# Rows and weights of a graph network turned by VectorE instead of TensorE

## The reference, cut to what matters

```python
# layers 0 and 3 (layer 1 alike, with x @ Wq + bq, no Wo and a mask)
q = x @ Wq.T; k = x @ Wk.T; v = x @ Wv.T + bv
p = softmax(q @ k.T * scale + bias)            # per head
x = layernorm(x + (p @ v) @ Wo.T + bo)
# layer 2, twice
attn = masked_normalised(softmax(h @ h.T / sqrt(D)) * adj)
ctx = (attn * upper) @ (h @ Wl.T) + diag(attn) * (h @ Ws.T) + (attn * lower) @ (h @ Wr.T)
h = relu(layernorm(ctx) * gain + shift)
```

## Time and profile before

| | before |
|---|---|
| median of 3 runs | 2714.04 us (2711.18 to 2718.5) |
| the profiled execution | 2714.95 us, span 2712.9 us |
| PE busy | 2558.7 us, 94% |
| DVE busy | 2079.0 us, 77% |
| ACT busy | 1498.6 us, 55% |
| POOL busy | 1804.6 us, 67% |
| rows turned on PE (L381, L1055), busy | 79.4 + 10.0 + 58.9 us |
| granted TensorE clock, mean | 0.978 |

### The profile page before, as it was taken

One profiled execution on the slowest core, in us unless ns is written; L12 is line 12 of the kernel. 1 busy time (PEld: TensorE's weight loads), 2 busy tenths in 40 slices (PEclk: granted clock), 3 DMA queues, 4 the chain that ended last, 5 costly groups with the idle time before them and its releaser, 6 DMA issues. The chain is left out here.

```text
span 2712.9 us, 65508 instructions
## 1 busy us (share of the span) xinstructions
PE 2558.7 (94%) x22558; PEld 2193.4 (81%) x22558; DVE 2079.0 (77%) x3594; ACT 1498.6 (55%) x3060; POOL 1804.6 (67%) x2045
## 2 busy tenths in 40 slices
PE   7999999996999999969999989999996999999997
PEld 6888888885878888768888878888885888888886
DVE  4788888884888888856666657888886588888887
ACT  4555555553666666535555545666664555555553
POOL 2767777772666666656666647888884567767776
PEclk9999999998999999979999999999998999999998
DMA  3222212213222222132122213232222122212211
GB/s 111 72 70 71 64 60 71 71 47 96 66 78 76 79 74 92 55 111 72 55 75 62 67 60 127 83 93 90 85 86 77 50 72 71 62 62 71 69 58 51
DMA packets 179475, 200.90 MB, mean 74 GB/s; under 512 B 56608, under 2 KB 179360, under 8 KB 179360
## 3 DMA queue, kind: packets, MB, share of 16 engines
q1 hardware_dynamic: 179360, 199.38, 23.6%
HBM read 136.42 MB, written 62.91 MB: 73 GB/s over the span
## 5 line engine op out<-in xcount | busy, mean ns | idle before, releaser
L1095 PE MATMUL l_ps_h<-l_w,l_hT 128*128 128x384 f32 x3456 | 660.3, 342 | 16.5 <-DVE l_hs L1299 14.8
L1095 PEld LDWEIGHTS l_ps_h<-l_w,l_hT 128*128 128x128 f32 x3456 | 592.8, 188 | 63.0 <-issue 33.1
L416 PE MATMUL l_ps_p<-l_xT,l_w 128*128 128x512 f32 x2304 | 604.7, 407 | 6.0 <-DVE l_xT L653 4.5
L343 POOL TENSOR_TENSOR l_pr<-l_sc,l_st 128x768 f32<-128x768 f32 x192 | 283.4, 1476 | 374.7 <-DVE l_st L691 364.3
L416 PEld LDWEIGHTS l_ps_p<-l_xT,l_w 128*128 128x128 f32 x2304 | 418.1, 190 | 95.3 <-ACT l_xT L545 5.3
L313 POOL TENSOR_TENSOR v<-v,l_bvs 128x768 f32<-128x768 f32 x192 | 375.9, 1958 | 0.0
L1182 ACT ACTIVATE l_hlr<-l_ps_h 64x384 f32<-64x384 f32 x512 | 248.7, 486 | 196.8 <-PE l_ps_h L1095 188.8
L698 DVE TENSOR_REDUCE l_st<-l_pr 128x12 f32<-128x768 f32 x192 | 182.8, 952 | 179.0 <-ACT l_pr L609 176.2
L410 PE MATMUL l_ps_p<-l_w,l_xT 128*128 128x384 f32 x1584 | 314.9, 344 | 1.8 <-ACT l_k L566 1.8
L576 ACT ACTIVATE v<-l_ps_p 64x192 f32<-64x192 f32 x704 | 228.9, 325 | 149.7 <-PE l_ps_p L410 142.6
L1003 POOL TENSOR_TENSOR l_hlr<-l_hlr,l_sides 128x768 f32<-128x768 f32 x128 | 243.9, 1905 | 85.0 <-ACT l_hlr L1182 85.0
(11 more groups left out here) (130 smaller groups left out, 4424.7 us busy)
## 6 DMA issues: line engine op xcount, KB each, us to landing
rows<-l_yo SPq DMA_DIRECT2D x256, 192.0 KB, 1.9
l_xa<-rows SPq DMA_DIRECT2D x64, 768.0 KB, 5.0
l_xr<-rows SPq DMA_DIRECT2D x192, 192.0 KB, 2.4
l_xa<-in_x SPq DMA_DIRECT2D x16, 768.0 KB, 4.9
l_xr<-in_x SPq DMA_DIRECT2D x64, 192.0 KB, 2.4
out<-l_yo SPq DMA_DIRECT2D x64, 192.0 KB, 1.9
l_edge<-in_adj SPq DMA_DIRECT2D x80, 128.0 KB, 2.3
raw<-in_L_gnn_Wq SPq DMA_DIRECT2D x3, 576.0 KB, 5.9
```

The costliest lines, as they stand in the source:

```text
L343: nc.gpsimd.tensor_tensor(pr[b][:, :, :], sc[b][:, :, :], st[b][:, 0, :].unsqueeze(2).to_broadcast([P, HEADS, NODES]), ALU.subtract).then_ ...
L416: last = nc.tensor.matmul(bank[:, :], W[m][:, l, t, o * P:(o + 1) * P], rows[:, r, t, :], start=c + t == 0, stop=c == 2 and t == KT - 1)
L1095: last = nc.tensor.matmul(ps_h[m][:, :D], hT[gpar][:, l, t, s * P:(s + 1) * P], W[m][:, r, t, :], start=c + t == 0, stop=c == 2 and t == K ...
```

## The change

The turning moves from TensorE to VectorE. VectorE turns blocks of 32x32, each within its own 32 partitions, so the transfer has to put the right block on the right partitions: partition 32a+c of `xa` takes, for k = 0 to 15, the quarter a of row 32k+c (96 numbers, 384 bytes). One VectorE instruction (`nc.vector.transpose`) on columns 32t to 32t+31 of all 16 k then gives tile t. Features are permuted by this; rows of the weights are permuted alike, which leaves products as they are.

- A group's load is four transfers of 192 KB (2048 runs of 384 bytes) instead of one of 768 KB (512 runs of 1536 bytes). There are two buffers `xa`; SP issues a load up to four (attention) or three (DiGCN) groups ahead, and no longer waits for TensorE.
- Attention: VectorE turns two tiles at the end of s = 0 and one at the end of s = 1 into an SBUF tile `xF`. ScalarE makes the high part from `xF` in s = 1 and s = 2. The low part is now made from two SBUF operands, at the end of s = 2 (two tiles) and s = 3 (one); in l1 by GpSimd, else by VectorE.
- DiGCN: VectorE writes `hF` itself (tile 2 in s = 0 for the next group, tiles 0 and 1 in s = 2 and 3 for the one after). ScalarE's plain copy is gone, and its high part reads `hF`.
- In DiGCN the end of attention step 2 (`attn`, `wide`) moves on VectorE from the end of s = 2 to s = 3, behind L1299.
- Weights: raw matrices come in four transfers each, for the turned ones in runs of 384 bytes, and are turned by VectorE into PSUM. Only Wo is still turned on TensorE, after the first ten projections. At a stage's start the projections wait per matrix.

Diff, cut to its core. Transfers and weights:

```diff
+def spread(src):
+    return src.rearrange("(i k c) (a f) -> i a c k f", k=4 * UNITS, c=32, a=4)
+def blocks(raw):
+    return raw[:, :, :].rearrange("p t n -> p (t n)").rearrange("p (k f) -> p k f", f=D // 4)
...
+                    part = mat.rearrange("(k c) (a f) -> a c k f", c=32, a=4)[a]
+                    sp.dma_start(blocks(self.raw[m])[q, :, :], part).then_inc(self.s_raw[m], 16)
```

In attention (tiles, tables, functions, then VectorE's unit and GpSimd's in l1):

```diff
-        xa = a.sb("xa", [P, UNITS, D])
+        xa = [a.sb(f"xa{b}", [P, 4 * UNITS, D // 4]) for b in range(2)]
+        xF = a.sb("xF", [P, KT, ROWS])
+        AHEAD = (("q", 0), ("q", 1), ("q", 2), ("k", 0), ("k", 1), ("k", 2), ("v", 0), ("v", 1), ("v", 2), ("v", 3))
+        BETWEEN = (((), (0,), (1,)), ((), (2,), (3,)), ((4,), (5,), (6,)), ((7,), (8,), (9,)))
+            def rows_in(g, gpar):
+                if counted(g - 1):
+                    sp.wait_ge(dve_turn, KT * (g - 1))
+                for j in range(4):
+                    sp.dma_start(xa[gpar][32 * j:32 * j + 32, :, :], src_x[g, j]).then_inc(s_xa[gpar], 16)
-            def rows_T(g, t, bank):
-                for u in range(UNITS):
-                    last = nc.tensor.transpose(bank[:, u * P:(u + 1) * P], xa[:, u, t * P:(t + 1) * P], ident[:, :])
-                last.then_inc(pe_x, 1)
+            def rows_turned(g, gpar, t):
+                dve.wait_ge(s_xa[gpar], 64 * (gpair(g, gpar) + 1))
+                if counted(KT * (g - 1) + t + 1):
+                    dve.wait_ge(act_x, KT * (g - 1) + t + 1)
+                    dve.wait_ge(low_x, KT * (g - 1) + t + 1)
+                nc.vector.transpose(xF[:, t, :], xa[gpar][:, :, 32 * t:32 * t + 32]).then_inc(dve_turn, 1)
+            def rows_low(g, gpar, t):
+                dve.wait_ge(act_x, KT * g + t + 1)
+                nc.vector.tensor_tensor(xT[gpar][:, 1, t, :], xF[:, t, :], xT[gpar][:, 0, t, :].bitcast(F32),
+                                        ALU.subtract).then_inc(low_x, 1)
...
                     softmax_sum(n, s)
-                    fill(i, par, s)
+                    for t in ((0, 1), (2,), (), ())[s]:
+                        rows_turned(i + 2, par, t)
+                    for t in ((), (), (0, 1), (2,))[s]:
+                        rows_low(i + 2, par, t)
...
+                        for t in ((), (), (0, 1), (2,))[s]:
+                            rows_low(i + 2, par, t)
```

In DiGCN, in turn on TensorE, ScalarE and VectorE (its start, then its unit):

```diff
-                pe.wait_ge(act_f, KT * (g + 1))
+                pe.wait_ge(dve_turn, KT * (g + 1))
...
-                    nc.scalar.activation(hF[gpar][:, t, :], bank[:, :], ACT.Copy).then_inc(act_f, 1)
-                    nc.scalar.activation(hT[gpar][:, 0, t, :], bank[:, :], ACT.Copy).then_inc(act_x, 1)
+                nc.scalar.activation(hT[gpar][:, 0, t, :], hF[gpar][:, t, :], ACT.Copy).then_inc(act_x, 1)
...
+            weights(LEFT)
+            for t in range(KT):
+                rows_turned(0, 0, t)
+            weights(RIGHT)
+            attention(0, 0, 0)
+            weights(SELF)
...
                     itself(n - 1, 1 - b)
+                    if s == 0:
+                        rows_turned(i + 1, 1 - par, 2)
+                    if s >= 2:
+                        rows_turned(i + 2, par, s - 2)
                     if s == 3:
                         attention(i + 1, 1 - par, 3)
+                        attention(i + 1, 1 - par, 4)
```

More of the change, by code:

```diff
@@ L87, in _ @@
             def _(sp):
-                self.load(sp, first_mats)
+                self.load(sp, first_mats, first_turned)
             @block.gpsimd
@@ L108, in _, with load @@
                     nc.vector.memset(self.v2[b][:, :, :, :], 0.0).then_inc(c_zero, 1)
-    def load(self, sp, mats, free=None):
+    def load(self, sp, mats, turned, free=None):
         for m, mat in enumerate(mats):
@@ L114, in load @@
                 free(m)
-            sp.dma_start(self.raw[m][:, :, :], mat.rearrange("(t p) n -> p t n", p=P)).then_inc(self.s_raw[m], 16)
-            self.loads[m] += 1
+            if m == 3:
+                sp.dma_start(self.raw[m][:, :, :], mat.rearrange("(t p) n -> p t n", p=P)).then_inc(self.s_raw[m], 16)
+                self.loads[m] += 16
+                continue
+            for a in range(4):
+                q = slice(32 * a, 32 * a + 32)
+                if turned:
+                    part = mat.rearrange("(k c) (a f) -> a c k f", c=32, a=4)[a]
+                    sp.dma_start(blocks(self.raw[m])[q, :, :], part).then_inc(self.s_raw[m], 16)
+                else:
+                    part = mat.rearrange("(a t r) n -> a r t n", a=4, r=32)[a]
+                    sp.dma_start(self.raw[m][q, :, :], part).then_inc(self.s_raw[m], 16)
+                self.loads[m] += 16
 class Pass:
@@ L644, in _, with weight_turned @@
             nc.vector.memset(bvs[:, :, :], 0.0).then_inc(c_zero, 1)
-            for step in range(steps):
+            def weight_turned(step):
+                m, t = divmod(step, KT)
+                if not transposed:
+                    return
+                dve.wait_ge(s_raw[m], loaded[m])
+                if step >= 4:
+                    dve.wait_ge(dve_w, step - 3)
+                nc.vector.transpose(w_bank(step)[:, :D], blocks(raw[m])[:, :, 32 * t:32 * t + 32]).then_inc(dve_wt, 1)
@@ L888, in _, with rows_in @@
         def _(sp):
-            sp.dma_start(xa[:, :, :], src_g[0]).then_inc(s_xa, 16)
+            def rows_in(g, gpar):
+                if not inside(g, groups):
+                    return
+                if counted(g - 1):
+                    sp.wait_ge(dve_turn, KT * (g - 1))
+                for j in range(4):
+                    sp.dma_start(xa[gpar][32 * j:32 * j + 32, :, :], src_x[g, j]).then_inc(s_xa[gpar], 16)
+            rows_in(0, 0)
+            rows_in(1, 1)
             sp.dma_start(edge[0][:, :, :], adj_g[0]).then_inc(s_edge[0], 16)
@@ L927, in group @@
                     store(n - 4, s)
-            over_groups(sp, groups, group)
+            over_groups(sp, groups, group, 2)
             if ends:
@@ L1208, in normed @@
                                          scale=ln[b][:, 20:21]).then_inc(act_y, 1)
-            rows_T(0, 0)
+            for step in range(KT):
+                weight_high(step)
+            for t in range(KT):
+                rows_high(0, 0, t)
+            for step in range(KT, 2 * KT):
+                weight_high(step)
             attention(0, 0, 1)
+            for step in range(2 * KT, steps):
+                weight_high(step)
             def group(i, pair, par):
```

366 lines of the change are left out of this document (196 added, 170 removed).

## The result

The changed kernel takes 2730.84 us (median of 5 runs, 2729.26 to 2732.55) against 2714.64 us (5 runs) of the kernel before on the same chip: 1.0058 times as long, 95% interval 1.0047 to 1.007. The forecast was 2694 us and faster; the time lies 0.8 us above the range.

The account below looks back on a forecast made before the run. TensorE was taken to bound l0, l3 and l20, TensorE plus the row-buffer transfer l1, VectorE l21. Terms -20 - 22 - 16 + 25 + 13 = -20 us gave 2695, by the median 2694 us; range 2650 to 2730.

Parts of the forecast that it names:

- Price of a turned tile: VectorE, all stages: turning a tile of 512 columns takes 0.68 us, three tiles 2.0 us a group.
- l20: First DiGCN stage, 15 groups: VectorE has room, TensorE gains all of its 1.05 us a group, 16 us shorter.
- l21: Second DiGCN stage, 14 groups: VectorE has no room, 1.8 us more a group, 25 us longer.
- Starts: Stage starts: +4.5 us each in l20 and l21, +3 in l0, +2 in l1, -1 in l3, together +13 us.
- Second price: l0 and l3: VectorE's low part with two SBUF operands waits out GpSimd's instruction under way, about 1.4 us a group.
- l0 and l3: Attention stages, 14 steady groups each: VectorE's waits take in 3.6 us against 3.4 needed; 0.7 us a group gained, 20 us.
- l1: Attention stage, 14 groups: TensorE could gain 1.05 + 1.0 us a group, 1.6 taken as GpSimd's slack is short; 22 us shorter.
- The rival at 2715: Low parts in l0 and l3 held up twice as long, nothing gained there, l21 loses as forecast: 2715 us, chance 0.17.

Follow-up runs that it names:

- l03_sum_behind: Changed kernel with turned tiles and low parts ahead of the sum that waits for the exponential, in l0 and l3: l0 620.4 us, l3 617.5, profiled execution 2696.99.
- before_add_first: Kernel before, with GpSimd's residual addition ahead of the value bias in l1: 2704.12 us, ratio 0.9958; l1 530.5 us.
- l1_add_first: Changed kernel with GpSimd's residual addition ahead of the value bias in l1: l1 531.2 us, 15.2 shorter.
- l1_sum_behind: Changed kernel with VectorE's turned tiles ahead of the sum that waits for the exponential, in l1 alone: l1 536.8 us, 9.6 shorter.
- combo: Changed kernel with turned tiles and low parts ahead of the sum, l1's addition ahead of value bias, small loads earlier, l21 undone: 2636.32 us, ratio 0.9716.
- the two experiments with 512: Changed kernel, l0's and l3's low part replaced by a one-SBUF-operand instruction, without and with tiles and low parts ahead of the sum: l0 middles 442.0 and 425.6 us.

## Why the prediction was wrong, point by point

- **Price of a turned tile**, 0.68 us: measured 0.69 in l0 and 0.70 in l21. The step that I called decisive was right. The estimate of 0.71 from the 311 ns of the Trainium skill (VectorE: DVE Perf Modes, The three transpose paths) is within 0.02 too.
- **l20**, 15 x 1.05 = 16 us: measured 18.1, or 1.28 a group. Right; TensorE gets back a little more than the starts of the earlier trace rows show.
- **l21**, +25: the middle grew by 19.2/12 = 1.60 us a group where I took 1.8; +22.8 with its start. Right, also in the mechanism (TensorE waits 22.9 us for VectorE's context, the place in the unit gives nothing back), though of the 3 us a group of waiting that I named one sees 2.
- **Starts**, +13: measured +7.4, with other shares. l0, l20 and l21 lost nothing. In l20 three tiles are turned from 6.3 us after the stage's start (1198.41 against 1192.11) and the first projection is at +11.7, so rows landed sooner than the 7.2 us I took. l1 lost 8.4 instead of 2: I had costed the row loads' landing, but not that VectorE's first instruction there waits for the small loads, which stand behind eight loads in SP's queue. Each queue that a step is put ahead in has to be asked who waits on what is behind.
- **Second price**, right: low parts of 1.11 us (forecast 1.0 to 1.2), the hold-up on the second one in s = 2 alone, 1.27 us for the 1.4 forecast, and VectorE's busy time in l0 44.6 us more over 13 groups, 3.4 a group as forecast. What it left out is that the hold-up of the small steps moves from L703 to L776 and grows by 0.16 us a unit, 0.65 a group.
- **l0 and l3**, -20: measured +9.5 beside their starts, that is from the first scores to TensorE's last product. This is the step that failed: "Of the latter some 1.5 us can't shrink ... 2.4 can. So 3.6 us can be taken in". The exponential's wait went from 51.1 to 28.3 us, 1.75 a group, not 2.4, and TensorE's 1.05 us saved a group became waiting: it is idle in 12.3 of 480 us. I counted a wait as room wherever the new work stands. But it stood behind the sum and the reciprocal, so it did not run during the wait; it delayed the next unit, and the wait shrank only as far as the delay passed through. l03_sum_behind puts the same work into the wait, and 17 and 18 us come back, some of it perhaps by the shorter hold-up of the small steps; both stages are then 12.8 and 14.5 us faster than before, more than the forecast's 10.
- **l1**, -22: measured -4.2 beside its start, 0.24 a group instead of 1.6. The failed step is "TensorE could gain 1.05 + 1.0 us", with GpSimd's slack in s = 2 as the only doubt. Behind the row buffer's wait lay a loop of VectorE and GpSimd of 7.8 us a unit. before_add_first shows that it was on l1's path before the change too, for at most 0.5 us a group in the middle; l1_add_first and l1_sum_behind show its two removable parts; combo shows that without them l1 reaches 29.0 us a group, 2.6 less than before. The row that could have told it was GpSimd's and VectorE's waits for each other in l1, which I didn't read, since TensorE's one wait seemed to explain its gaps.
- **The rival at 2715** (low parts held up twice as long, l0 and l3 gain nothing) came nearest in its outcome, by luck and not by its mechanism (the low parts were held up as forecast); none had l1 in it. The terms of the sum missed by +29.5 in l0 and l3, +17.8 in l1, -2 in l20, -2.4 in l21 and -5.6 in the starts: 37 us in all, which is the gap between 2694 and 2731.

## What to carry to other kernels

A wait on an engine is room only for work that stands ahead of the waiting instruction in its queue, and that is ready then; the same instructions behind it are covered only in part (in l0, 1.75 us a group of the exponential's wait where 2.4 were counted on). Before a wait of the bounding engine is booked as a gain, look for a loop among the other engines of nearly the same period: if removing the named wait, or moving the late producer, only renames it, the loop is the bound. In a shared queue, whatever doesn't belong to the loop (a bias wanted two units later, loads for a later group) goes behind what does.

## What the runs showed that I had not expected

- VectorE's TENSOR_SCALAR with a single SBUF input is held up by GpSimd as well: 0.29 us free and 1.94 on average (L743, 256 columns), 0.85 and 1.24 us on average in the two experiments with 512, where a free one takes 0.43. The turned tile, also with one SBUF input, is not: 687 ns mean in a stage where GpSimd is busy in 353 of 480 us.
- Hold-ups hit short instructions by luck of place: twelve columns took 0.17 or 0.77 us, as they came after GpSimd's bias addition or into it, and the change moved the hold-up from one small step to another. A mean that grows (L776) has to be read with its neighbour that shrinks (L770).
- Four loads of 192 KB in runs of 384 bytes, eight issued back to back, left the starts of l0, l20 and l21 within 0.1 us of what they were, all changes there taken together.
